# Two FFN and two cross-attention layers on one core: the same steps in another written-out order

## The chip, the core and the metric

The kernel runs on one core of a Trainium2 chip, in one launch. The metric is the device time in microseconds, the median of several runs. TensorE (PE) does the matrix products, VectorE (DVE) and ScalarE (ACT) read PSUM and do element-wise work, GpSimd (POOL) does element-wise work on SBUF alone, and SyncE (SP) issues nearly all transfers. Each engine takes its instructions strictly in the order in which the program lists them; engines meet only through semaphores.

## The reference, cut to what matters

The input x is (16, 128, 128): 16 sequences of 128 tokens with 128 channels, and ctx has the same shape. Four residual layers follow each other, each scaled by the tanh of a gain:

```python
x = x + tanh(g_xattn[0]) * L0_xattn(ctx, ctx, layernorm(x))   # 16 heads of 8, softmax over the heads
x = x + tanh(g_ffn[0])   * L0_ffn(layernorm(x))               # 8 experts of 256, top 2, computed densely
x = x + tanh(g_xattn[1]) * L1_xattn(layernorm(x), ctx)        # both-way attention, then one linear layer
x = x + tanh(g_ffn[1])   * L1_ffn(layernorm(x))               # ternary weights, 8-bit activations, 512 inner
```

## The kernel before

The 16 sequences go in 8 pairs (c from 0 to 7). For every pair the stages are the same, and three or four pairs are in work at a time. The steps have names of the form engine.step, with a number n where a pair has several.

- **First attention (a).** `sp.load_a` loads x and ctx; `dve.a_stats`, `pool.a_rstd` (L843 to L848) and `act.a_norm` normalize; `pe.kq` projects (n = 0 keys, n = 1 queries), after `dve.qkv_lo` and `dve.a_xlo` have made the low parts of the operands. Keys and queries are split into three bf16 parts (`act.part1`, `dve.part_rest`, `act.part2`, `pool.part3` L869), written to DRAM (`sp.store_parts` L791) and fetched back in another layout (`sp.fetch_rows` L799). Four units u follow: `pe.scores`, `dve.head_max`, `dve.head_shift`, `act.head_exp`, `pool.head_sum` (L939, a tree of four additions; two units of pair 0 do it on DVE, L1598), `dve.head_inv`, `pool.head_norm` (L945, in place), then `pe.weighted_v` and `pe.out`.
- **Experts (m).** 16 tiles k: `pe.up` (six matmuls, L1188 to L1190), `act.m_tanh`, `dve.m_u`, then `dve.m_h` or, for the seven odd tiles up to 13, `pool.m_h` (L876); per expert `pe.down` (L1448) and the sum into y (`act.y` with `pool.y` L904 for two experts, `dve.y` for six). m_h is a ring of four buffers.
- **Second attention (f).** A chain of small steps: `dve.f_stats`, `pool.f_rstd`, `act.f_norm`, `pe.f_ct`, `act.f_ct`, `pe.f_scores`, `dve.f_max`, `act.f_exp`, `dve.f_ainv`, `act.f_an`, `pe.f_at`, `act.f_at`, `dve.f_max_max`, `act.f_exp_max`, `pe.f_c2q`, `act.f_c2q`, `pool.f_prod` (L925), `act.f_w4`, `pe.f_z`, `dve.x3`; `pool.y_res` (L912) prepares the residual.
- **Last FFN (g).** `dve.g_stats`, `pool.g_rstd`, ... `act.g_pr`, `act.g_pt`, `pe.g_down`, `act.o_raw`, `pool.out` (L917), `sp.store` (L814).

Once, at the start: weights are loaded (`sp.w_out` is five transfers, the last of them wo_t, L760; then `sp.w_moe`, `sp.w_ffn`, `sp.w_fin`, `sp.w_late`), split into high and low parts (`act.w_hi`, `pool.w_lo`, `dve.w_lo` L1511), and `act.th` (L974) takes the tanh of the gains. `act.th` waits for all five transfers of `sp.w_out`; `dve.bias_parts` (eight instructions, L1521 to L1532) waits for `act.th`. `pe.warm_s`, `pe.warm_f` and `pe.warm_g` are spare matmuls whose results nobody reads.

The order is written out by hand in two tables, WHEN (per pair) and ONCE: every step has a number, and each engine issues its steps in the order of these numbers. The numbers are used for nothing else:

```python
def order(engine):
    ...
    return [(step, n, c) for _, step, n, c in sorted(steps)]
...
for now in order("pool"):
    ...
    if p := due(now, "pool.m_h", n):
```

Of the kernel before, what the change touches and what calls it, by code (L numbers as in the profile page):

```python
# [47 lines left out]
    "sp.load_a": (12, 1501, 2546, 3638, 7464, 12475, 17304, 20931),  # L48
    "sp.store_parts": (
# [6 lines left out]
    ),  # L56
    "sp.fetch_rows": (
        (1960, 3826, 7126, 11165, 15185, 19034, 23535, 27447),
        (2176, 3979, 7280, 10827, 14847, 18694, 23197, 27600),
    ),  # L60
    "sp.load_res": (2646, 5144, 9928, 12576, 16625, 22383, 25012, 28949),
    "sp.load_f": (2697, 11318, 15338, 19216, 24905, 27785, 31537, 34931),
    "sp.store": (16288, 20577, 24859, 28736, 32637, 36238, 38259, 39516),
    "pool.a_rstd": (467, 2292, 3414, 4828, 11299, 16757, 20361, 24484),
    "pool.ct_lo": (399, 2108, 2915, 8603, 12228, 13500, 20286, 21743),
    "pool.part3": (
        (1032, 2533, 6643, 10304, 14257, 18449, 22272, 26895),
        (1821, 3535, 7016, 10717, 14736, 18386, 23086, 27337),
    ),
    "pool.head_sum": (  # L70
# [4 lines left out]
    ),  # L75
    "pool.head_norm": (
# [14 lines left out]
    ),  # L91
    "pool.top_probs": (6705, 10149, 14319, 18585, 22334, 26625, 30788, 33972),
    "pool.y_res": (10367, 13574, 18312, 21817, 25821, 29981, 33448, 36784),
    "pool.f_rstd": (9408, 13378, 17534, 21621, 25895, 30055, 33522, 36662),
    "pool.f_prod": (11082, 15324, 19402, 23525, 27788, 31830, 34983, 37677),
    "pool.g_rstd": (12106, 15779, 20090, 24057, 28227, 32433, 35617, 38044),
    "pool.out": (16206, 20488, 24778, 28655, 32555, 36140, 38177, 0),
    "pool.y": (
        (7460, 11150, 14873, 19328, 23451, 27713, 31905, 34557),
        (7541, 11421, 15250, 19479, 23600, 27862, 32053, 35058),  # L100
    ),
    "act.a_norm": (619, 2451, 3543, 6806, 12380, 17209, 20836, 24936),
# [1712 lines left out]
```

## Time and profile before

| | before |
|---|---|
| time, median of 3 runs | 399.9 us (399.1 to 401.47) |
| span of the profiled execution | 397.3 us |
| what lies around the span, against the median | 2.6 us |
| busy: PE, DVE, POOL, ACT | 82%, 79%, 75%, 65% of the span |
| chain that ended last: PE, POOL, DVE, issue, ACT | 37%, 25%, 13%, 10%, 7% |
| mean granted clock of PE | 0.948 |

The span runs from the first to the last instruction. A busy share is an average over the whole span; the pairs overlap, so the start (until the first scores at 27.7 us), the middle and the end (the last pair alone) have different limits and have to be read apart. The numbers in WHEN and ONCE are in hundredths of a microsecond by their size: the last store has 39516, and the span is 397.3 us.

### The profile page before, as it was taken

The numbers are of one execution on the slowest core, as the hardware profiler recorded it, in microseconds if no ns is written. First come the engines' busy times: TensorE is split into PE (matmuls) and PEld (weight loads), VectorE is DVE, ScalarE is ACT, GpSimd is POOL, SyncE is SP. The second block draws the span as 40 slices with busy tenths as digits, with TensorE's granted clock in tenths as the row PEclk, the third lists the DMA queues.
The fourth block names the chain that finished last, engine by engine and source line by source line (L and its number), as shares of the span: only waits on it lengthen the run. The fifth ranks groups of instructions, "written<-read, shape, count | busy, mean of one in ns | idle before, by whom it ended". The sixth has DMA issues, their size and how long they took to land.

```text
span 397.3 us, 10407 instructions
## 1 busy us (share of the span) xinstructions
PE 324.9 (82%) x3326; PEld 284.0 (71%) x3326; DVE 313.1 (79%) x913; ACT 256.4 (65%) x726; POOL 299.1 (75%) x459
## 2 busy tenths in 40 slices
PE   1365589898999789979998899879978997996875
PEld 1255469787898679867986698669957896994742
DVE  2679877598869997999799979995989678778434
ACT  4335254536846797779667885777658855875754
POOL 4378989799898989898999799988778873443010
PEclk9999767999999999999999999998999999999585
DMA  5967210300341114012401221204100000000000
GB/s 161 289 192 210 81 36 21 116 17 16 88 115 34 29 41 128 19 56 63 108 15 47 68 87 29 61 6 131 33 16 1 28 15 2 2 29 14 2 13 13
DMA packets 34454, 24.17 MB, mean 61 GB/s; under 512 B 3617, under 2 KB 32097, under 8 KB 34401
## 3 DMA queue, kind: packets, MB, share of 16 engines
q1 hardware_dynamic: 33680, 23.32, 19.7%
q8 instruction: 27, 0.44, 0.5%
q10 hardware_dynamic: 720, 0.20, 0.2%
q14 instruction: 27, 0.21, 0.2%
HBM read 16.16 MB, written 7.34 MB: 59 GB/s over the span
## 4 chain that ended last, share of the span: by engine, by line
PE 37%; POOL 25%; DVE 13%; issue 10%; ACT 7%; DMA 4%; SPq 3%; POOLq 0%; DVEq 0%; ACTq 0%
POOL tree L939 9%; PE ps_d L1448 8%; POOL attn L945 8%; PE ps_z L1188 4%; PE ps_a L1196 3%; PE ps_z L1189 3%; PE ps_z L1190 3%; POOL m_h L876 2%; DVE head_max L1584 2%; DMA wf_raw<-in_wd 2%; DVE m_u L1623 1%; DMA k_rows<-rows_dram 1%; DVE y L1655 1%; PE ps_sc L1234 1%; DVE shifted L1590 1%
## 5 line engine op out<-in xcount | busy, mean ns | idle before, releaser
L1188 PE MATMUL ps_z<-m_xhi,w_hi 128*128 128x256 f32 x240 | 76.9, 320 | 12.7 <-DVE m_h L1631 6.1
L945 POOL TENSOR_TENSOR attn<-attn,head_inv 128x1024 f32<-128x1024 f32 x32 | 75.8, 2371 | 0.2 <-DVE head_inv L1606 0.2
L1448 PE MATMUL ps_d<-wdn,m_h 128*128 128x128 f32 x512 | 71.4, 283 | 4.7 <-DVE m_h L1631 2.1
L1448 PEld LDWEIGHTS ps_d<-wdn,m_h 128*128 128x128 f32 x512 | 63.1, 194 | 8.5 <-issue 4.1
L1189 PE MATMUL ps_z<-m_xhi,w_lo 128*128 128x256 f32 x240 | 68.8, 287 | 0.0
L1190 PE MATMUL ps_z<-m_xlo,w_hi 128*128 128x256 f32 x240 | 68.6, 286 | 0.0
L1623 DVE SCALAR_TENSOR_TENSOR m_u<-m_tanh,ps_z 128x256 f32<-128x256 f32 x120 | 49.0, 411 | 17.6 <-ACT m_tanh L1033 16.7
L1033 ACT ACTIVATE m_tanh<-ps_z 128x256 f32<-128x256 f32 x120 | 45.9, 384 | 26.0 <-PE ps_z L1190 25.6
L1188 PEld LDWEIGHTS ps_z<-m_xhi,w_hi 128*128 128x128 f32 x240 | 46.7, 195 | 19.3 <-issue 6.1
L876 POOL TENSOR_TENSOR m_h<-m_u,m_z 128x256 f32<-128x256 f32 x56 | 41.1, 734 | 17.2 <-DVE m_u L1623 17.2
L939 POOL TENSOR_TENSOR tree<-tree 128x256 f32<-128x256 f32 (+2 forms) x90 | 46.4, 515 | 7.1
L1189 PEld LDWEIGHTS ps_z<-m_xhi,w_lo 128*128 128x128 f32 x240 | 46.9, 196 | 0.0
L1190 PEld LDWEIGHTS ps_z<-m_xlo,w_hi 128*128 128x128 f32 x240 | 46.7, 195 | 0.0
L939 POOL TENSOR_TENSOR tree<-attn 128x512 f32<-128x512 f32 x30 | 38.3, 1277 | 6.5 <-ACT attn L1046 6.3
L1584 DVE TENSOR_REDUCE head_max<-ps_sc 128x64 f32<-128x1024 f32 x32 | 38.9, 1215 | 4.5 <-PE ps_sc L1234 4.2
L1046 ACT ACTIVATE attn<-shifted 128x1024 f32<-128x1024 f32 x32 | 33.7, 1055 | 10.1 <-DVE shifted L1590 10.1
L1590 DVE TENSOR_TENSOR shifted<-ps_sc,head_max 128x1024 f32<-128x1024 f32 x32 | 38.8, 1213 | 0.3
L1655 DVE SCALAR_TENSOR_TENSOR y<-ps_d,weights,y 128x128 f32<-128x128 f32 x96 | 28.8, 342 | 4.5 <-PE ps_d L1448 3.1
L1631 DVE TENSOR_TENSOR m_h<-m_u,ps_z 128x256 f32<-128x256 f32 x67 | 27.6, 414 | 5.8 <-PE ps_d L1448 5.1
L1031 ACT ACTIVATE m_z<-ps_z 128x256 f32<-128x256 f32 x53 | 20.2, 381 | 14.6 <-PE ps_z L1190 13.8
L1196 PE MATMUL ps_a<-attn,v_diag 128*32 128x128 f32 x512 | 20.4, 290 | 3.7 <-POOL attn L945 3.3
L1234 PE MATMUL ps_sc<-q_rows,k_rows 48*128 48x64 bf16 x512 | 13.7, 196 | 7.7 <-DVE shifted L1590 5.6
(311 smaller groups left out, 852.0 us busy)
## 6 DMA issues: line engine op xcount, KB each, us to landing
rows_dram<-qk_parts SPq DMA_DIRECT2D x16, 192.0 KB, 2.2
k_rows<-rows_dram SPq DMA_DIRECT2D x16, 192.0 KB
q_rows<-rows_dram SPq DMA_DIRECT2D x16, 192.0 KB
w_raw<-in_w SPq DMA_DIRECT2D x2, 1024.0 KB, 7.9
rows_dram<-qk_parts SPq DMA_DIRECT2D x16, 128.0 KB, 2.0
x_in<-in_x SPq DMA_DIRECT2D x8, 128.0 KB, 2.4
ct_in<-in_ctx_t SPq DMA_DIRECT2D x8, 128.0 KB, 2.4
rows_dram<-qk_parts SPq DMA_DIRECT2D x16, 64.0 KB, 1.7
```

What stands on the lines that cost most here:

```text
L876: pool.tensor_tensor(m_h[:, k % 4], m_u[:, k % 4], m_z1[:, n % 3], ALU.mult).then_inc(s_mhp, 1)
L939: pool.tensor_tensor(dst, src[:, 0:n, :], src[:, n:2 * n, :], ALU.add).then_inc(s_tree, 1)
L945: pool.tensor_tensor(e, e, head_inv[:, u % 2].unsqueeze(1).to_broadcast([P, HEADS, HALF]), ALU.mult).then_inc(s_attn, 1)
L1033: act.activation(m_tanh[:, k % 2], tile_bank(p, k)[:, 0:TOK], ACT.Tanh, scale=0.5).then_inc(s_mt, 1)
L1046: act.activation(attn[:, b, :, k0:k0 + HALF], shifted[:, u % 2], ACT.Exp).then_inc(s_exp, 1)
L1188: pe.matmul(dst, hi_w, hi_x, start=start, stop=False)
L1189: pe.matmul(dst, lo_w, hi_x, start=False, stop=False)
L1190: return pe.matmul(dst, hi_w, lo_x, start=False, stop=True)
L1448: last = pe.matmul(ps_d[:, b * P:(b + 1) * P], m_h[:, m % 4, b * P:(b + 1) * P], wdn[:, m], start=(k == 0), stop=(k == TPE - 1))
L1584: dve.tensor_reduce(head_max[:, u % 2], sc.rearrange("p h k -> p k h"), AX.X, ALU.max).then_inc(s_hmax, 1)
L1590: dve.tensor_tensor(shifted[:, u % 2], sc, head_max[:, u % 2].unsqueeze(1).to_broadcast([P, HEADS, HALF]), ALU.subtract).then_inc(s_shift, 1)
L1623: dve.scalar_tensor_tensor(m_u[:, k % 4], m_tanh[:, k % 2], 1.0, z[:, 0:TOK], ALU.add, ALU.mult).then_inc(s_mu, 1)
```

## The change

Only the numbers in WHEN and ONCE change. Every step, wait, buffer and instruction is kept; on each of the five engines the same list of steps (101 on SP, 226 on POOL, 490 on ACT, 517 on PE, 689 on DVE) is sorted into another order. In words, as far as the prediction speaks of it:

- Start: `act.th` stands ahead of `act.qkv_hi` n = 0 and `act.a_norm` of pair 0, and `dve.bias_parts` ahead of `dve.qkv_lo` n = 0 and 2 and of `dve.a_xlo`. Queries are projected ahead of keys. `sp.w_fin` and `sp.w_late` move behind the fetches of pair 0 and pair 1. On POOL, `pool.a_rstd` of pair 2 and `pool.part3` of pair 1 no longer stand between the first `pool.head_sum` and the first `pool.head_norm`. `dve.w_lo` n = 1 moves from 57.52 to 70.11.
- Middle, on POOL: `pool.part3` of pair 3 (both) and `pool.y_res` of pair 0 stand between `pool.m_h` n = 1 and n = 2 of pair 1; in pairs 3 and 4 a `pool.head_sum` stands between them; `pool.head_norm` n = 3 of pair 6 stands ahead of `pool.m_h` n = 4 of pair 5 and of `pool.g_rstd` of pair 4, behind which it stood.
- End: `act.g_pr` n = 0 and `act.g_tanh` n = 3 of pair 6 move behind `act.f_exp` of pair 7.
- Spare matmuls: seven of `pe.warm_s` at the very start, none between `pe.weighted_v` n = 0 of pair 0 and the middle of that pair's `pe.up`; seven of `pe.warm_f` directly behind the last `pe.down`, none between them and `pe.f_z` of pair 7.

```diff
 WHEN = {
...
     "pool.part3": (
-        (1032, 2533, 6643, 10304, 14257, 18449, 22272, 26895),
-        (1821, 3535, 7016, 10717, 14736, 18386, 23086, 27337),
+        (1641, 2949, 6053, 10610, 13579, 17418, 21932, 25191),
+        (1572, 2879, 6193, 10693, 13881, 18505, 22649, 25857),
     ),
     "pool.head_sum": (
-        (3117, 4949, 8301, 12302, 16280, 20570, 24852, 28729),
-        (0, 5624, 9105, 13076, 17232, 21319, 25518, 29679),
-        (3829, 6030, 9761, 13649, 17656, 21891, 26017, 30177),
-        (0, 7157, 10779, 14947, 18951, 23148, 26958, 31135),
+        (3251, 5069, 8653, 12419, 16440, 20294, 24398, 28083),
+        (0, 5762, 9296, 13163, 17127, 21313, 25260, 28946),
+        (3864, 6263, 9939, 14022, 17677, 22217, 25551, 29499),
+        (0, 7490, 10976, 14686, 18658, 23025, 26992, 30406),
     ),
     "pool.head_norm": (
...
-        (4596, 7995, 11800, 15901, 19859, 24178, 28349, 32128),
+        (4622, 8086, 11783, 15578, 19989, 23740, 27517, 31236),
     ),
     "pool.m_h": (
...
-        (6861, 10441, 14516, 18511, 22765, 26821, 31061, 34325),
-        (7078, 10515, 14799, 18778, 22945, 27399, 31522, 34691),
-        (7615, 11224, 15399, 19254, 23676, 27936, 31979, 35147),
-        (7921, 11495, 15704, 19785, 23982, 28011, 32359, 35331),
+        (6944, 10468, 14543, 18361, 22146, 26375, 30193, 33154),
+        (7208, 10834, 15060, 18948, 22578, 26779, 30264, 33493),
+        (7348, 11407, 15202, 19352, 22869, 26921, 30860, 34201),
+        (7781, 11712, 15812, 19775, 23668, 27750, 31470, 34272),
...
-    "pool.y_res": (10367, 13574, 18312, 21817, 25821, 29981, 33448, 36784),
+    "pool.y_res": (10763, 14472, 18574, 21123, 26628, 29237, 33635, 35725),
...
-    "pool.g_rstd": (12106, 15779, 20090, 24057, 28227, 32433, 35617, 38044),
+    "pool.g_rstd": (12017, 15885, 19657, 23550, 27822, 31541, 34593, 36830),
...
-    "sp.store": (16288, 20577, 24859, 28736, 32637, 36238, 38259, 39516),
+    "sp.store": (16084, 20898, 24336, 28603, 32313, 35876, 37263, 38278),
...
 ONCE = {
...
-    "sp.w_fin": 1005,
...
-    "sp.w_late": 2804,
...
-    "act.th": 851,
...
-    "dve.qkv_lo": (957, 467, 1010),
-    "dve.w_lo": (2176, 5752),
...
-    "dve.bias_parts": 1030,
...
+    "sp.w_fin": 2403,
...
+    "sp.w_late": 4120,
...
+    "act.th": 487,
...
+    "dve.qkv_lo": (910, 463, 929),
+    "dve.w_lo": (2501, 7011),
...
+    "dve.bias_parts": 511,
...
```

## Rows read from the trace of the kernel before

**Rows 1.** Busy time in one stretch of the middle: us, PE, PEld, DVE, ACT, POOL; clock, DMA.
```profile
216.00:256.00 40.00, 36.20 (x391) 31.97 (x390) 35.90 (x110) 30.18 (x90) 36.16 (x55) 1.00 0.22 65
```

**Rows 2.** Busy time of POOL alone in two stretches: length, busy, PE's clock, DMA.
```profile
65.00:270.00 205.00, 186.31 (x281) 1.00 0.20 57
270.00:292.00 22.00, 16.60 (x25) 0.92 0.24 70
```

**Rows 3.** POOL's waits from 46 to 320 us: in total, times, longest us.
```profile
POOL m_h L876 <- DVE m_u L1623: 6.0, 5, 1.8
POOL tree L939 <- ACT attn L1046: 5.1, 7, 1.1
POOL qk_parts L869 <- ACT qk_parts L1022: 3.6, 2, 2.2
```

**Rows 4.** Timeline of SP's queue at the start: start us, us, issue.
```profile
3.66 0.43 SPq L760 DMA_DIRECT2D wo_t<-in_wo  x1
...
21.54 1.35 SPq L799 DMA_DIRECT2D q_rows<-rows_dram  x2
```

**Rows 5.** The tile wo_t, its transfer from issue to landing.
```profile
DMA to landing us min/median/max: 4.8/4.8/4.8
```

**Rows 6.** Timeline of DVE in the start: start us, us, instruction.
```profile
10.26 0.69 DVE L1521 TENSOR_SCALAR bias_raw<-bias_raw,th 96x128 f32<-96x128 f32 x1
...
12.41 0.42 DVE L1532 TENSOR_TENSOR bias_parts<-bias_rest,bias_mid 1x256 bf16<-1x256 f32 x1
...
37.65 1.97 DVE L1598 TENSOR_REDUCE tree<-attn 128x64 f32<-128x1024 f32 x1
...
58.52 1.39 DVE L1511 TENSOR_TENSOR w_lo<-w_raw,w_hi 128x1024 fp32r<-128x1024 f32 x1
```

**Rows 7.** Timeline of PE in the start.
```profile
14.41 0.52 PE L1188 MATMUL ps_a<-a_xhi,wqkv_hi 128*128 128x256 f32 x1
...
27.65 0.46 PE L1234 MATMUL ps_sc<-q_rows,k_rows 48*128 48x64 bf16 x16
```

**Rows 8.** Timeline of POOL in the first attention stage.
```profile
31.80 1.26 POOL L939 TENSOR_TENSOR tree<-attn 128x512 f32<-128x512 f32 x1 [1.28 <-ACT attn L1046]
33.15 1.66 POOL L939 TENSOR_TENSOR tree<-tree 128x256 f32<-128x256 f32 x3
...
36.61 2.37 POOL L945 TENSOR_TENSOR attn<-attn,head_inv 128x1024 f32<-128x1024 f32 x1
...
58.90 2.53 POOL L939 TENSOR_TENSOR tree<-tree 128x256 f32<-128x256 f32 x3
```

**Rows 9.** Timeline of POOL in the middle; in brackets idle time before, and releaser.
```profile
107.76 0.74 POOL L876 TENSOR_TENSOR m_h<-m_u,m_z 128x256 f32<-128x256 f32 x1 [1.01 <-DVE m_u L1623]
...
188.70 0.73 POOL L876 TENSOR_TENSOR m_h<-m_u,m_z 128x256 f32<-128x256 f32 x1 [1.31 <-DVE m_u L1623]
...
228.48 0.73 POOL L876 TENSOR_TENSOR m_h<-m_u,m_z 128x256 f32<-128x256 f32 x1 [1.37 <-DVE m_u L1623]
...
279.98 0.73 POOL L876 TENSOR_TENSOR m_h<-m_u,m_z 128x256 f32<-128x256 f32 x1 [1.80 <-DVE m_u L1623]
281.53 0.19 POOL L843 TENSOR_TENSOR g_rs<-g_mv,eps_col 128x2 f32<-128x2 f32 x1 [0.82 <-DVE g_mv L1493]
...
282.75 2.39 POOL L945 TENSOR_TENSOR attn<-attn,head_inv 128x1024 f32<-128x1024 f32 x1
```

**Rows 10.** Busy time of PE in two stretches: length, busy (matmuls), granted clock, DMA.
```profile
55.10:65.30 10.20, 9.67 (x60) 0.50 0.11 33
65.30:270.10 204.80, 180.87 (x1964) 1.00 0.20 57
```

**Rows 11.** Timeline of DVE in the last pair's second attention.
```profile
368.44 0.22 DVE L1693 SCALAR_TENSOR_TENSOR f_m<-ps_f,bsum,f_nmax 128x1 f32<-128x1 f32 x1
```

**Rows 12.** Timeline of ACT there.
```profile
369.08 0.35 ACT L1096 ACTIVATE f_a<-ps_f,f_nmax 128x128 f32<-128x128 f32 x1
```

**Rows 13.** Timeline at the end: the last two stores, issued by SP.
```profile
394.83 0.82 SPq L814 DMA_DIRECT2D out<-o_sb  x2
```

More of the change, by code:

```diff
@@ L102 @@
-    "act.a_norm": (619, 2451, 3543, 6806, 12380, 17209, 20836, 24936),
-    "act.ct_hi": (340, 2055, 2534, 8320, 9723, 13339, 17931, 21368),
-    "act.a_xhi": (822, 2871, 5804, 9918, 13310, 17762, 21810, 26364),
+        (7279, 10905, 14989, 19020, 22718, 26708, 30709, 33715),
+        (7419, 11336, 15131, 19162, 22798, 26850, 30789, 34130),
+    ),
+    "act.a_norm": (679, 1837, 5049, 8518, 12383, 16339, 19913, 24167),
+    "act.ct_hi": (336, 1457, 2864, 6835, 9864, 14678, 18099, 22144),
+    "act.a_xhi": (848, 2108, 5725, 9636, 13059, 17093, 21630, 24955),
@@ L126 @@
+    "act.m_norm": (5563, 9071, 12939, 16897, 20950, 24847, 28730, 32242),
+    "act.m_xhi": (5697, 9275, 13155, 17043, 21066, 24982, 28807, 32635),
     "act.m_tanh": (
[16 rows of a table removed]
-    ),
-    "act.top_exp": (6437, 9981, 14327, 18048, 22233, 26566, 30878, 34125),
-    "act.f_norm": (9540, 13614, 17679, 21946, 26051, 30231, 33652, 36792),
-    "act.f_ct": (9759, 13840, 17967, 22153, 26222, 30453, 33841, 36918),
-    "act.f_exp": (10217, 14157, 18330, 22490, 26492, 30766, 34200, 37176),
-    "act.f_an": (10363, 14349, 18511, 22640, 26775, 31003, 34336, 37309),
@@ new lines @@
+    "act.top_exp": (6420, 10017, 14188, 17914, 21975, 26063, 29783, 32886),
+    "act.f_norm": (9789, 13587, 17614, 21321, 25208, 29448, 32809, 35734),
+    "act.f_ct": (9942, 13741, 17783, 21555, 25515, 29587, 32984, 35823),
+    "act.f_exp": (10258, 14030, 18131, 22015, 25894, 29882, 33347, 36012),
+    "act.f_an": (10363, 14200, 18240, 22176, 26003, 29991, 33505, 36094),
+    "act.f_at": (10526, 14413, 18445, 22339, 26167, 30154, 33681, 36194),
+    "act.f_exp_max": (10649, 14793, 18653, 22559, 26196, 30280, 33778, 36245),
@@ L156 @@
+    "act.f_c2q": (11026, 15029, 18930, 22868, 26503, 30523, 34014, 36406),
+    "act.f_w4": (11127, 15247, 19103, 23040, 27045, 30930, 34130, 36466),
+    "act.g_norm": (12144, 16013, 20163, 23677, 27949, 31719, 34782, 36957),
+    "act.g_r": (12489, 16243, 20337, 24374, 28239, 31986, 34910, 37168),
+    "act.g_qt": (13032, 16825, 20786, 25014, 28484, 32319, 35198, 37315),
     "act.g_tanh": (
[4 rows of a table removed]
[4 rows of a table added]
     ),
     "act.g_pr": (
-        (14413, 18108, 22704, 27012, 30533, 34037, 37029, 38752),
-        (15510, 19430, 23653, 27490, 31635, 35192, 37774, 39102),
+        (14442, 17925, 22897, 26797, 30729, 33204, 36532, 37585),
+        (15160, 19248, 23255, 27104, 31018, 34189, 36782, 37907),
@@ L209 @@
     "pe.up": (
[16 rows of a table removed]
[16 rows of a table added]
     ),
-    "pe.gate": (5784, 9616, 13576, 17651, 21651, 25789, 30049, 33850),
+    "pe.gate": (6006, 9403, 13995, 17239, 21528, 25265, 29318, 32740),
     "pe.down": (
[8 rows of a table removed]
-    ),
-    "pe.f_ct": (9683, 13767, 17883, 22050, 26149, 30375, 33765, 36851),
-    "pe.f_scores": (9978, 13938, 18062, 22280, 26317, 30548, 33989, 36991),
-    "pe.f_at": (10437, 14429, 18637, 22942, 26854, 31083, 34431, 37359),
-    "pe.f_c2q": (10839, 14988, 19118, 23275, 27450, 31440, 34833, 37574),
[8 rows of a table added]
+    ),
@@ L242 @@
+    "pe.f_ct": (9898, 13695, 17737, 21437, 25300, 29541, 32921, 35788),
+    "pe.f_scores": (10077, 13831, 17872, 21695, 25703, 29681, 33091, 35891),
+    "pe.f_at": (10435, 14324, 18356, 22251, 26078, 30065, 33593, 36140),
+    "pe.f_c2q": (10915, 14918, 18783, 22696, 26392, 30411, 33903, 36330),
     "pe.f_z": (
-        (11234, 15326, 19457, 23614, 27702, 31672, 35092, 37700),
-        (11293, 15401, 19532, 23745, 27931, 32016, 35224, 37805),
+        (11319, 15512, 19178, 23127, 27347, 30950, 34257, 36462),
+        (11365, 15559, 19225, 23173, 27394, 31004, 34304, 36555),
@@ new lines @@
+    "dve.f_max": (10188, 13959, 18025, 21926, 25823, 29810, 33216, 35958),
+    "dve.f_ainv": (10343, 14165, 18218, 22142, 25981, 29969, 33434, 36064),
+    "dve.f_max_max": (10569, 14610, 18582, 22493, 26211, 30198, 33726, 36228),
+    "dve.f_q2c": (11005, 15167, 19061, 22942, 26552, 30888, 34045, 36312),
+    "dve.x3": (11521, 15758, 19427, 23330, 27550, 31165, 34466, 36690),
+    "dve.g_amax": (12255, 16105, 20261, 24016, 28086, 31855, 34874, 37049),
+    "dve.g_clamp": (12302, 16138, 20294, 24049, 28118, 31888, 34907, 37082),
```

182 lines of the change are left out of this document (82 added, 100 removed), and 250 rows, old and new, of the table WHEN.

## The prediction, on record before the changed kernel ran

> **What bounds the kernel now.** I read the busy time by stretches first, because the shares of the whole span mix a start, a middle and an end with different limits. In the middle a pair costs about 40 us, and in such a stretch PE, DVE and POOL are each busy for 36 of the 40 us [rows 1]; ACT is not. So no engine alone is the limit. Three engines at 90% hand work to each other through small rings of buffers, and what an order can save is the remaining tenth. Next I read POOL alone: 186.3 us of 205.0 before 270 us (91%), but only 16.6 of 22.0 (75%) from there to 292 us [rows 2]. That is the worst place of the middle. Then POOL's waits from 46 to 320 us: the largest is `m_h`, which waits for DVE's `m_u`, 6.0 us in 5 times [rows 3]. In the timeline I looked up what stood behind POOL at each of them, since that is what an order can put in front. Outside the middle, the start until the first scores and the last pair's chain are read step by step. The clock comes last: PE runs at full clock through the middle and at half from 55.1 to 65.3 us [rows 10].
>
> The rows are of an execution with a span of 397.3 us. The median of the runs shown is 399.9 us, so 2.6 us are taken as lying around the span, before and after alike. I sum differences, and add them to 399.9. With runs from 399.1 to 401.5, 0.5% (2.0 us) is about what can be told from no change.
>
> **The change, part by part.** No instruction goes or comes, so each part is a wait that ends earlier or later.
>
> *Start, until the scores.* `act.th` waits for wo_t, issued at 3.66 us and landed 4.8 us later, at 8.5 [rows 4, 5]. The transfers ahead of it on SP are the same in both orders. ACT now stands at this wait with `a_norm` behind it, and DVE with `bias_parts`, and behind that the low parts that both projections need. `bias_parts` lasts from 10.26 to 12.83 us, 2.6 us [rows 6]; from about 8.7 on that ends at 11.3. Three short DVE steps of about 0.3 us each (estimate, by the last rows of `bias_parts`) end at 12.2. From the start of the queries' projection to the queries' fetch it took 21.54 - 14.41 = 7.1 us [rows 4, 7]. Now the keys, which were far ahead before, go through the same path together with the queries: one more projection, four more steps of ACT, DVE and POOL, three more stores. Their cost lies between nothing and another 7.1 us; I take 3.4, about half, since the two share each engine by turns. The queries' fetch is issued at 12.2 + 7.1 + 3.4 = 22.7 us instead of 21.54. Scores follow it by 27.65 - 21.54 = 6.1 us [rows 4, 7]: 28.8 us, +1.2. The moved `w_fin` cannot give this back, because the stores now wait for the parts and not for SP's queue.
>
> *From the scores to the end of pair 0's attention.* The first tree went from 31.80 to 33.15 + 1.66 = 34.8 us, but `head_norm` began only at 36.61 [rows 8], since two other steps of POOL stood between. They are moved away, and the 1.2 us are won back there. The two sums on DVE take 1.97 us each [rows 6]; with the later start the second `head_norm` waits for the first of them, about 0.5 us. So +0.5 at the end of this stage. The steps that were moved away must still be done: they go where POOL was waiting for ACT's exponentials, a wait of 0.9 us among those of [rows 3]. I take +0.7 for the start as a whole; the bounds are -2.2 (the keys cost nothing) and +4.9 (they cost 7.1).
>
> *The port.* While DVE subtracted `w_lo` (58.52, 1.39 us [rows 6]), POOL's three additions from 58.90 took 2.53 us; the same three took 1.66 us elsewhere [rows 8]. That is 0.9 us, and POOL had work waiting behind. The new order puts this subtraction after the first expert tiles, near a pause of POOL. I take -0.9, bounds 0 and -0.9. The Trainium skill (SBUF — State Buffer, section "Who interferes with whom") says that a DVE instruction with two SBUF inputs and a GpSimd instruction that reads SBUF exclude each other, the later one waiting for the whole of the earlier; the rows agree. By that rule the 0.9 us go only if the subtraction meets a true pause of POOL, and otherwise move to another POOL step; then this term is 0 and the sum below ends at 395.8. In the middle no large DVE step has two SBUF inputs, since they read PSUM, so nothing more is to be had there.
>
> *The middle.* Four places, each a wait of `m_h` on DVE. In pair 5, POOL waited 1.80 us at `m_h` and 0.82 us at `g_rstd`, with `head_norm` (2.39 us) standing behind both [rows 9]. The new order puts `head_norm` ahead of both, and it fits into the 2.6 us almost exactly: -2.6. In pairs 1, 3 and 4 the waits are 1.01, 1.31 and 1.37 us, 3.7 together [rows 9]. What is put in front there is longer than the wait (a whole tree, two parts and a residual), so `m_h` and with it `pe.down` come later, and PE and DVE, themselves busy for 90%, lose a part of what POOL wins. I take half, -1.8. Bounds for the middle: 0, if PE and DVE bring back every wait elsewhere, and -14.7, the sum of the three rows of [rows 3]. I stay at -4.4, nearer to the first, because only these places could be traced to a swap. What the other moved steps do there I put at 0 for want of a row; it lies within these bounds.
>
> *The end.* In pair 7 `f_m` of the first half was ready at 368.44 + 0.22 = 368.66 us, and `f_exp` began at 369.08 [rows 11, 12], because `g_pr` and `g_tanh` of pair 6 stood in front on ACT. They move behind it: -0.4. The rest of the chain is the same small steps, each waiting for the one before. Bounds: +1.0 (below) to -3.
>
> *PE's clock.* The granted clock was at half from 55.1 to 65.3 us although spare matmuls stood in front [rows 10]; the new order has none between the first `weighted_v` and the middle of the first experts, and none in the last pair's chain before `f_z`. A matmul took 9.67 / 60 = 0.16 us of PE at half clock and 180.87 / 1964 = 0.09 at full [rows 10], with somewhat different mixes. If `f_ct` and `f_scores` also run at half, the last chain gains about 1 us of length. I take 0 for both places, since the dense `up` matmuls brought the clock back by themselves at 65.3. The Trainium skill (TensorE: Matmul & The Clock Gate, section "HAM oscillation — how this bites in real kernels") says that a gap in PE's work puts the clock back to half, so that the next burst starts slowly. That speaks against this change.
>
> **The sum:** +0.7 - 0.9 - 4.4 - 0.4 = -5.0 us, and 399.9 - 5.0 = 394.9 us.
>
> **The rivals.**
> - *The whole order works as its numbers read.* They are sort keys and no measurement, and no term above comes from them. But the last store had the key 39516, and the trace issued it within 394.83 to 395.65 us [rows 13]; the new key is 38278, 12.4 us less: 387.5 us. This needs all of POOL's named waits in the middle (14.7 us in [rows 3]) to shrink by most of their length, and the start not to be late. For it: 90% on three engines leaves that much room. Against it: the start, where the key of `act.th` (4.87 us) lies ahead of the landing at 8.5.
> - *The waits come back on the other engines.* Where a tree of 3.0 us [rows 8] fills a wait of 1.31 or 1.37 us, `m_h` is 1.7 and 1.6 us later than before; in pair 1 it is 1.1, with three steps of about 0.7 us (estimate, by the 0.74 of `m_h`) in a wait of 1.01. That is 4.4 us in all, and it reaches the end as far as the ring of four buffers has no slack. If half does, the three places give +2.2 in place of -1.8, and the sum is 394.9 + 4.0 = 398.9 us: the same within 0.5%. For it: PE and DVE at 90% [rows 1]. Against it: PE had no long wait there that is put down to POOL.
> - *Slower: the half clock lasts longer.* Place: from the first `weighted_v` to the middle of pair 0's experts, where no spare matmuls are left. At 0.16 - 0.09 = 0.07 us for each matmul, 100 more matmuls at half clock cost 7 us, and 399.9 - 5.0 + 7.0 = 401.9 us. It decides from about 100 matmuls, near two thirds of pair 0's `up` and `down`. For it: the clock was low there even with the spare matmuls [rows 10]. Against it: the dense experts raised it before.
>
> **How the numbers follow.** My forecast (390.5 to 397.9, all faster by over 0.5%) has a chance of 0.44, the whole order 0.24, the returning waits 0.20, the slow clock 0.12. Faster by over 0.5%: 0.44 + 0.24 = 0.68; within 0.5%: 0.20; slower: 0.12. The predicted time is that of the likeliest, 394.9 us. The range goes from 387.0, just below the whole order's 387.5, to 401.5, which leaves out about half of the slow-clock case and what may lie under the whole order's time: some 0.15 together. The forecast's own range is 390.5 to 397.9.
>
> **What would show it right or wrong.** Start: `act.th` near 8.5 us, `bias_parts` until 11.3, the first scores near 28.8; scores at 27.7 or earlier would refute the term. Port: DVE's second `w_lo` beside a pause of POOL, and no tree addition group of 2.5 us. Middle: POOL from 270 to 292 us as dense as before 270; `m_h` waits under 3 us in all; if instead PE's waits for `m_h` grow, the second rival is right. End: `f_exp` directly behind `f_max`. Clock: the first full-clock stretch of pair 0's experts beginning near 65 us; at 72 or later, the third rival. The prediction is wrong if the pairs of the middle come to 39 us or less each (the whole order), or if the start loses more than 2 us and the middle gains nothing.

## The result, and the profile after

The new order is slower: 417.25 us (runs of 413.76 to 419.14) against 399.5 us of the kernel before on the same chip, a ratio of 1.0439 with a 95% interval of 1.0395 to 1.0484. The forecast was 394.9 us, and the range ended at 401.5.

The page first: engine, busy us, share of the span, instructions. The upper fence is the kernel before, the lower the one after.

```profile
PE 324.9 (82%) x3326; PEld 284.0 (71%) x3326; DVE 313.1 (79%) x913; ACT 256.4 (65%) x726; POOL 299.1 (75%) x459
```
```profile
PE 329.8 (80%) x3323; PEld 291.0 (70%) x3326; DVE 328.4 (79%) x913; ACT 257.4 (62%) x726; POOL 296.3 (72%) x459
...
PEclk9996558889999989999999899999999999999688
...
PE 52%; DVE 23%; issue 11%; ACT 9%; POOL 2%; DMA 1%; SPq 1%; DVEq 0%; ACTq 0%; POOLq 0%
```

Two things stand out. DVE's 913 instructions are busy for 15.3 us longer, though an order can't make an instruction longer by itself. Added up one by one they are 10.5 us longer (377.6 us against 367.1); the rest of the 15.3 us is that neighbours overlap less. And in the slices from 31 to 62 us the clock is at 5 and 6 tenths. In the chain of waits POOL fell from 25% to 2%: it is no longer what the others wait for.

Where the time goes is seen from one step that each pair does once, the statistics after its experts (the first `f_st` in DVE's timeline), in us from the start of the span:

| pair | 0 | 1 | 2 | 3 | 5 | 7 |
|---|---|---|---|---|---|---|
| before | 94.6 | 133.6 | 172.9 | 213.4 | 297.7 | 363.4 |
| after | 103.1 | 149.0 | 191.0 | 231.7 | 315.4 | 381.0 |
| later by | 8.5 | 15.4 | 18.1 | 18.3 | 17.7 | 17.6 |

The whole loss is made in pairs 0, 1 and 2. From there on the lag neither grows nor shrinks.

Nearly all of DVE's growth is in a handful of small instructions. Groups by line (busy us, mean ns), before and then after:

```profile
L1664 DVE TENSOR_SCALAR w_first<-expert_no,top_nof,tprob 128x8 f32<-128x8 f32 x16 | 4.9, 303 | 0.4 <-POOL tprob L894 0.4
L1664 DVE TENSOR_SCALAR w_second<-expert_no,top_nof,tprob 128x8 f32<-128x8 f32 x16 | 4.5, 282 | 0.0
```
```profile
L1664 DVE TENSOR_SCALAR w_second<-expert_no,top_nof,tprob 128x8 f32<-128x8 f32 x16 | 9.0, 562 | 0.0
L1664 DVE TENSOR_SCALAR w_first<-expert_no,top_nof,tprob 128x8 f32<-128x8 f32 x16 | 7.9, 492 | 0.0
...
L1750 DVE TENSOR_SCALAR g_q<-g_r 128x256 bf16<-128x256 f32 (+1 forms) x9 | 4.9, 557 | 1.8 <-ACT g_r L1143 1.5
...
L1645 DVE CAST top_nof<-top_no 128x16 f32<-128x16 uint32 x8 | 3.4, 421 | 0.0
```

L1664 works on 8 columns, and takes 16.9 us in place of 9.4. The timeline of pair 0's four of them shows why. DVE after, then POOL after:

```profile
74.49 1.48 DVE L1664 TENSOR_SCALAR w_first<-expert_no,top_nof,tprob 128x8 f32<-128x8 f32 x1
75.89 0.78 DVE L1664 TENSOR_SCALAR w_second<-expert_no,top_nof,tprob 128x8 f32<-128x8 f32 x1
76.58 0.77 DVE L1664 TENSOR_SCALAR w_first<-expert_no,top_nof,tprob 128x8 f32<-128x8 f32 x1
77.27 0.28 DVE L1664 TENSOR_SCALAR w_second<-expert_no,top_nof,tprob 128x8 f32<-128x8 f32 x1
77.46 1.21 DVE L1511 TENSOR_TENSOR w_lo<-w_raw,w_hi 128x1024 fp32r<-128x1024 f32 x1
```
```profile
73.57 2.37 POOL L945 TENSOR_TENSOR attn<-attn,head_inv 128x1024 f32<-128x1024 f32 x1
75.90 1.43 POOL L876 TENSOR_TENSOR m_h<-m_u,m_z 128x256 f32<-128x256 f32 x2
79.56 0.73 POOL L904 TENSOR_TENSOR y<-y_raw,x 128x256 f32<-128x256 f32 x1 [2.23 <-ACT y_raw L1074]
```

The first ends at 75.97, just behind `attn` (75.94); the second and the third end one `m_h` apart (76.67, 77.35), as POOL's two instructions do. The fourth meets an idle POOL and takes 0.28 us. So each of these instructions waits for the POOL instruction that is running, and three of them in a row wait three times. (The wait lies inside the instruction's own time and not at a semaphore: that engines meet only through semaphores, as said ahead of the prediction, does not hold here.) In the kernel before, the same four took 0.28 us each, from 70.89 on, and POOL stood idle just then, from 70.27 to 72.47. DVE's first of the four, and POOL's next instruction:

```profile
70.89 0.28 DVE L1664 TENSOR_SCALAR w_first<-expert_no,top_nof,tprob 128x8 f32<-128x8 f32 x1
...
72.47 0.68 POOL L869 TENSOR_TENSOR qk_parts<-qk_rest,qk_parts 128x256 bf16<-128x256 f32 x1 [2.20 <-ACT qk_parts L1022]
```

This is the longest of the `qk_parts` waits of [rows 3]. The new order did away with it, and so with the gap that DVE's small steps had been using. The chain of waits runs through them: start us, us, what.

```profile
73.50 1.08 DVE shifted L1590
74.57 1.40 DVE w_first L1664
75.97 0.69 DVE w_second L1664
76.67 0.69 DVE w_first L1664
...
78.60 0.17 DVE weights L1669
...
79.12 0.37 ACT y_raw L1074
...
79.62 2.06 PE ps_d L1448 x8
```

PE's second `down` product waits for it, and then takes 2.06 us for 8 products; at 87.32 the same takes 0.89. That is the clock, read from the stretches (us, PE, PEld, DVE, ACT, POOL busy with counts, granted clock, DMA):

```profile
34.87:65.59 30.72, 20.99 (x235) 16.87 (x237) 22.85 (x38) 11.27 (x22) 25.07 (x30) 0.50 0.31 91
65.59:79.24 13.65, 8.42 (x99) 7.55 (x93) 11.18 (x28) 7.23 (x20) 9.28 (x14) 1.00 0.42 116
79.24:86.07 6.83, 5.77 (x25) 5.54 (x26) 1.72 (x5) 1.25 (x4) 4.72 (x7) 0.50 0.00 0
...
216.00:256.00 40.00, 34.37 (x377) 31.48 (x375) 35.46 (x102) 29.42 (x87) 33.37 (x51) 0.96 0.21 60
```

At half (1.2 GHz) are 30.7 us in one piece, in place of two pieces of 6.8 and 10.2 before [rows 10 for the second]; and another 6.8 in the middle of pair 0's experts, which begins while PE stands idle for 2.5 us, until that `down` product starts at 79.62. In the stretch of [rows 1] POOL has 33.37 of 40 us where it had 36.16.

The other marks that the prediction named. The start, on SP and on PE:

```profile
22.00 1.35 SPq L799 DMA_DIRECT2D q_rows<-rows_dram  x2
```
```profile
24.44 5.02 PE L1213 MATMUL ps_f<-ident_bf 128*128 128x128 bf16 x56
29.39 0.41 PE L1234 MATMUL ps_sc<-q_rows,k_rows 48*128 48x64 bf16 x16
```

`act.th` ran at 8.50, `bias_parts` ended at 10.98 (11.3 was expected), the queries' fetch is issued at 22.0 (22.7 expected; 21.54 in [rows 4]), and the scores come at 29.39 (28.8 expected; 27.65 in [rows 7]), straight behind 14 groups of four spare products.

POOL's waits, from 46 to 338 us, beside [rows 3]; and pair 5's place, beside [rows 9]:

```profile
POOL m_h L876 <- DVE m_u L1623: 7.6, 5, 3.4
POOL tree L939 <- ACT attn L1046: 6.6, 5, 1.4
POOL y L904 <- ACT y_raw L1074: 6.0, 5, 2.2
```
```profile
300.76 0.73 POOL L876 TENSOR_TENSOR m_h<-m_u,m_z 128x256 f32<-128x256 f32 x1
301.45 0.20 POOL L843 TENSOR_TENSOR g_rs<-g_mv,eps_col 128x2 f32<-128x2 f32 x1
```

Pair 5's two waits are gone, as traced: both steps follow `attn` with no idle time in brackets. But `m_h` waits longer in all than before, where under 3 us was expected, and a wait of `y` for ACT has come up that was not there. PE's waits for `m_h`, the sign of the second rival, add up to 9.2 us in place of 8.5 (6.9 in the first experiment below): no growth that would carry this loss. At the end `f_exp` stands directly behind `f_max`, as expected: it waits for `f_m` alone (beside [rows 11, 12]).

```profile
386.28 0.37 ACT L1096 ACTIVATE f_a<-ps_f,f_nmax 128x128 f32<-128x128 f32 x1 [0.62 <-DVE f_m L1693]
```

### The profile page after: what moved, and what is told of

It reads as the page before. It is cut to its first block, busy times and chain, and to the rows that moved or that the text cites. A ratio compares the mean times of both kernels' runs of the same rounds, so it can differ in the third digit from the quotient of the medians.

```text
span 413.9 us, 10404 instructions
## 1 busy us (share of the span) xinstructions
PE 329.8 (80%) x3323; PEld 291.0 (70%) x3326; DVE 328.4 (79%) x913; ACT 257.4 (62%) x726; POOL 296.3 (72%) x459
## 4 chain that ended last, share of the span: by engine, by line
PE 52%; DVE 23%; issue 11%; ACT 9%; POOL 2%; DMA 1%; SPq 1%; DVEq 0%; ACTq 0%; POOLq 0%
PE ps_d L1448 13%; PE ps_z L1188 7%; PE ps_z L1189 5%; PE ps_z L1190 5%; DVE head_max L1584 3%; DVE shifted L1590 2%; DVE y L1655 2%; DVE m_u L1623 2%; DVE m_h L1631 2%; PE ps_a L1196 2%; PE ps_sc L1234 2%; DVE w_second L1664 1%; DVE w_first L1664 1%; PE ps_f L1213 1%; DMA wo_t<-in_wo 1%
## 5 line engine op out<-in xcount | busy, mean ns | idle before, releaser
L1448 PE MATMUL ps_d<-wdn,m_h 128*128 128x128 f32 x512 | 72.8, 287 | 9.4 <-ACT y_raw L1074 5.4
L1448 PEld LDWEIGHTS ps_d<-wdn,m_h 128*128 128x128 f32 x512 | 64.7, 198 | 13.1 <-issue 10.1
L1189 PE MATMUL ps_z<-m_xhi,w_lo 128*128 128x256 f32 x240 | 69.7, 291 | 0.0
L1190 PE MATMUL ps_z<-m_xlo,w_hi 128*128 128x256 f32 x240 | 69.5, 290 | 0.0
L1623 DVE SCALAR_TENSOR_TENSOR m_u<-m_tanh,ps_z 128x256 f32<-128x256 f32 x120 | 48.2, 412 | 15.7 <-ACT m_tanh L1033 14.9
L939 POOL TENSOR_TENSOR tree<-tree 128x256 f32<-128x256 f32 (+2 forms) x90 | 45.4, 504 | 7.1
L1189 PEld LDWEIGHTS ps_z<-m_xhi,w_lo 128*128 128x128 f32 x240 | 47.8, 199 | 0.0
L1190 PEld LDWEIGHTS ps_z<-m_xlo,w_hi 128*128 128x128 f32 x240 | 47.7, 199 | 0.0
L1655 DVE SCALAR_TENSOR_TENSOR y<-ps_d,weights,y 128x128 f32<-128x128 f32 x96 | 28.8, 341 | 4.1 <-PE ps_d L1448 3.5
```

Of the source, the lines that this page charges most:

```text
L939: pool.tensor_tensor(dst, src[:, 0:n, :], src[:, n:2 * n, :], ALU.add).then_inc(s_tree, 1)
L1189: pe.matmul(dst, lo_w, hi_x, start=False, stop=False)
L1190: return pe.matmul(dst, hi_w, lo_x, start=False, stop=True)
L1448: last = pe.matmul(ps_d[:, b * P:(b + 1) * P], m_h[:, m % 4, b * P:(b + 1) * P], wdn[:, m], start=(k == 0), stop=(k == TPE - 1))
L1623: dve.scalar_tensor_tensor(m_u[:, k % 4], m_tanh[:, k % 2], 1.0, z[:, 0:TOK], ALU.add, ALU.mult).then_inc(s_mu, 1)
L1655: dve.scalar_tensor_tensor(y[:, b], ps_d[:, b * P:(b + 1) * P], weights[:, b, n:n + 1], y[:, b], ALU.mult, ALU.add).then_inc(s_y, 1)
```

## The experiments

Four candidates for 17.7 us: the port (DVE's and POOL's instructions in each other's way at SBUF), PE's clock, the start, and the order as such (what stands in front of what, port and clock aside). Ratios are to the kernel before, run beside each on the same chip (398.2 to 399.0 us); the one of after is 1.0439, and 0.01 is 4 us.

**The port alone.** If L1664 waits because its form takes a port that POOL needs too (where this theory comes from is said further down), then another form should not wait. The only edit is the shape: 3 rows of 3 with a gap are read, and 9 in a row are written; the sum behind it reads 8 of the 9. `w_second` gets the same shape as `w_first`. The ninth column is no expert and is not used.

```diff
-        expert_no = sb("expert_no", [P, EXPERTS])
+        expert_no = sb("expert_no", [P, 3, 4])
-        w_first = sb("w_first", [P, 2, EXPERTS])
+        w_first = sb("w_first", [P, 2, 9])
-            pool.iota(expert_no[:], pattern=[[1, EXPERTS]], base=0, ...
+            pool.iota(expert_no[:], pattern=[[3, 3], [1, 4]], base=0, ...
-                            dve.tensor_scalar(dst[:, b], expert_no[:], ...
+                            dve.tensor_scalar(dst[:, b], expert_no[:, :, 0:3], ...
```

> The order of after, with the 32 instructions of L1664 in another form: the expert numbers lie in 3 rows of 3 with a gap (9 columns read instead of 8), so that the operand read and the operand written differ in shape and the instruction needs one SBUF port instead of two. Nothing else differs. Port theory: in after, L1664 took 16.9 us against 9.4 before, single ones 1.3 to 1.5 us against 0.28, because DVE waited for POOL's instruction to end; the chain of waits runs through them. They then take about 0.29 us each again, 9.5 us in all, and 4 to 7.5 of the 17 us come back: 410 to 413 us. Rival, order alone: DVE's lost time there is slack, and the time stays at 416 to 418 us though L1664 is short. If L1664 stays near 0.53 us on the mean, the shape is not what takes the second port and the run tells nothing of the price.

Measured: 410.33 us, ratio 1.0288 (1.0248 to 1.0329).

```profile
L1664 DVE TENSOR_SCALAR w_first<-expert_no,top_nof,tprob 128x9 f32<-128x9 f32 x16 | 4.4, 273 | 0.0
L1664 DVE TENSOR_SCALAR w_second<-expert_no,top_nof,tprob 128x9 f32<-128x9 f32 x16 | 4.4, 272 | 0.0
```

The subtraction behind them, in DVE's timeline:

```profile
75.44 1.78 DVE L1511 TENSOR_TENSOR w_lo<-w_raw,w_hi 128x1024 fp32r<-128x1024 f32 x1
```

All 32 take 0.27 us now, and 1.5 points of the 4.4 are gone. The subtraction, still with two SBUF inputs, takes 1.78 in place of 1.21 us: it inherits a part of the wait. The clock can have given little of this: in the trace it is at half for 30.7 us between 36 and 71 us, as in after for 30.7, and near 80 us for 3.4 in place of 6.8. The port theory holds, with its size. That the form matters through a port, and not in another way, is the theory's reading; the runs show the wait and that the form ends it.

**The same form in the old order**, as a control.

> The order of before, untouched, with L1664 alone in the one-port form (no spares added). A control for the form: in the order of before these instructions waited 0.4 us in all, so if the gain of 6.9 us in the order of after came from the port and not from the form as such, nothing changes here: 398 to 399.5 us, ratio 0.995 to 1.003. If the form gains by itself, it is under 396.

Measured: 397.94 us, ratio 0.9992 (0.9963 to 1.0021). No change: the form itself gains nothing where little collides, so the gain above comes from the collisions.

**The late half of the weights.** `w_lo` ran between the weights and their sum (77.46).

```diff
-    "act.w_hi": (1962, 1518, 6249, 1612),
+    "act.w_hi": (1962, 1518, 5430, 1612),
-    "dve.w_lo": (2501, 7011),
+    "dve.w_lo": (2501, 5850),
```

> The order of after with two steps moved back: the high half of the up weights on ACT from key 62.5 to 54.3 (after its v_diag of pair 1) and the low half on DVE from key 70.1 to 58.5 (after the a_xlo of pair 2). In after the low half ran at 77.46 between weights (end 77.55) and the sum of the weights (78.60), for which ACT's y and the second down product waited. Theory that this step is a part of the loss: pair 0's second half of experts starts 1.2 us earlier or more (up8 81.1 or before, in place of 82.3), and 1 to 2.5 us of it last to the end: 414.5 to 416 us. Rival, DVE is not late there: 417 us. Slower would mean that the moved steps now stand before the first products of pair 0's experts.

Measured: 415.97 us, ratio 1.0414 (1.0354 to 1.0475), within the interval of after. `w_lo` ran at 62.80, but the weights began 1.5 us later (76.01) and collided with POOL as before:

```profile
62.80 1.36 DVE L1511 TENSOR_TENSOR w_lo<-w_raw,w_hi 128x1024 fp32r<-128x1024 f32 x1
...
76.01 1.49 DVE L1664 TENSOR_SCALAR w_first<-expert_no,top_nof,tprob 128x8 f32<-128x8 f32 x1
77.41 0.78 DVE L1664 TENSOR_SCALAR w_second<-expert_no,top_nof,tprob 128x8 f32<-128x8 f32 x1
```

That theory falls by its mark: up8 started at 81.95, 0.4 us earlier and not 1.2. The time lies in the range given for it, but also in that of no change.

**The clock.** 70 more groups of spares (4 products each) in PE's gaps, in the order of after:

```diff
-    "pe.warm_s": (271, ..., 9876),
+    "pe.warm_s": tuple(sorted((271, ..., 9876) + (3149,) * 9 + (3398,) * 12 + (4225,) * 14 + (4524,) + (4683,) * 2
+        + (4956,) * 3 + (5040, 5168) + (5652,) * 5 + (5701,) * 2 + (6297,) * 4 + (6610,) * 2 + (6760,) * 4 + (7215,) * 10)),
```

> The order of after plus 70 more groups of spare products on PE (4 of 128 columns each) between 31.5 and 72.2 of the key time, so that PE has work in its gaps there. Clock theory: in after the granted clock was half from 34.87 to 65.59 us and from 79.24 to 86.07; with the gaps filled it is full in most of the first stretch, each product of 0.21 us there takes 0.14 or less, and 2.5 to 5 us come back: 412 to 414.5 us. Rival: the products of that stretch wait for DVE and POOL anyway, the clock changes and the time stays within 1 us of 417; or the spares stand in the way and it is slower.

Measured: 409.88 us, ratio 1.0284 (1.0239 to 1.0328). That is more than the 2.5 to 5 us expected. L1664 still takes 16.9 us. The clock is full throughout both stretches, and pair 0's statistics come at 96.4 in place of 103.1 us:

```profile
34.87:65.59 30.72, 26.81 (x455) 23.37 (x453) 25.22 (x46) 14.09 (x29) 27.67 (x34) 1.00 0.38 106
...
79.24:86.07 6.83, 6.79 (x69) 6.13 (x68) 5.61 (x12) 3.03 (x9) 6.59 (x7) 1.00 0.01 2
```

Where the 6.7 us arise, from the two traces: the first weighted values start at 45.62 in both, so up to there the full clock, net of the spares in front, gave nothing. At the statistics ahead of the experts this kernel is 1.6 us ahead (54.52 against 56.10), at the first `up` 2.9 (59.46 against 62.38), and the experts give the other 3.8.

**The old spares in their old places**, none added.

```diff
-    "pe.warm_s": (271, ..., 4224, 6759, 8188, 9130, 9152, 9831, 9853, 9876),
+    "pe.warm_s": (2027,) * 5 + (2769,) * 2 + (3083,) * 5 + (3396,) * 3 + (3744,) * 7 + (4245,) * 13 + (4683,)
+        + (5928,) * 2 + (6297,) * 4 + (7306, 7687, 9152, 9831, 9853, 9876),
```

> The order of after, with its 48 groups of spare products not added to but put back in front of the steps that they stood in front of in before (13 ahead of the first weighted_v, 1 ahead of its third, 2 ahead of pair 1's last scores, 4 ahead of up4). Clock theory in the narrow form (it is the moved spares that cost): the clock is full again for part of 35 to 65 us, and 3 to 7 us come back: 410 to 414 us. Rival: moved spares alone change little, since the real products are also spread otherwise: 416 to 418 us.

Measured: 419.06 us, ratio 1.0525 (1.0462 to 1.0589). No gain, and slower than either case of the expectation. The clock did change:

```profile
34.87:44.30 9.43, 6.36 (x100) 5.99 (x96) 8.69 (x13) 2.62 (x3) 7.63 (x7) 1.00 0.27 72
44.30:64.80 20.50, 15.72 (x156) 12.03 (x157) 13.76 (x25) 7.90 (x19) 16.24 (x22) 0.50 0.37 104
78.50:85.30 6.80, 5.60 (x27) 5.33 (x28) 2.00 (x7) 1.63 (x5) 4.20 (x6) 0.50 0.00 0
```

9.4 us of pair 0's attention at full clock bought nothing; what stayed at half was the rest of that attention and the first experts (`up` from 61.79). So putting the moved spares back is not enough. That the real products are also spread otherwise, and the old number of spares no longer fills the gaps, is argued; the run fits it.

**Pairs 0 and 1 by the old keys, the others by the new** (shifted by 1.2 us).

> Pairs 0 and 1 and all that is done once by the keys of before, pairs 2 to 7 by those of after (shifted by 1.2 us to join them). The lag of after behind before at the statistics that follow the experts was 8.5 us in pair 0, 15.4 in pair 1, 18.1 in pair 2 and 17.6 in pair 7. Theory that the loss is made in the first two pairs (the start, the port, the clock there): about 15 of the 17 us are gone, 400 to 403 us. Rival, the new order is worse in every pair and the first ones only show it first: each of six pairs loses some 2 us and it is 408 us or more. If the new order of the later pairs gains by itself, it is under 399 us.

Measured: 429.51 us, ratio 1.0786 (1.0748 to 1.0825), worse than either order. Pair 0, by its old keys, was 8.7 us late at its statistics, and L1664 took 13.5 us in all. The joint is a third order with losses of its own, which were not followed up, and the run tells nothing of the two.

**Port and clock together.**

> The order of after with both edits: the 32 instructions of L1664 in the form that needs one SBUF port (alone: 410.3 us, 6.9 us less than after on the median) and the 70 added groups of spare products (alone: 409.9, 7.4 less). If port and clock are separate losses they add up: 14 us back, 402 to 404 us. If each was the cover of the other (the chain waits for whichever is later), it stays at 407 us or more.

Measured: 406.18 us, ratio 1.0213 (1.0140 to 1.0286). Alone they gave back 1.51 and 1.55 points, together 2.26: less than the sum of 3.06, and more than either, but the interval reaches those of each alone. In the executions that were traced, the lag at pair 7's statistics is 17.6 us in after, 11.8 with the form, 11.2 with the spares and 6.1 with both, nearly the full sum (11.5 of 12.3 us). Whether the two add up in full or in part stays open.

**And the start.** Added to that: `act.th` at key 851 and `bias_parts` at 1030, as in the old table.

> As the kernel with both edits, and also the two steps of the start by the keys of before: act.th (the five small transfers, wo_t last at 8.5 us) behind the first a_xhi, and dve.bias_parts behind the first a_xlo. In after ACT's a_norm of pair 0 was 2.3 us later than before and the first scores 1.7 us later. Theory that the start is a third loss that lasts: 1.2 to 1.7 us less than with both edits alone, first scores at 28 us or earlier. Rival: the first scores wait for pair 0's fetched rows, later by another reason, and nothing changes.

Measured: 404.29 us, ratio 1.0169 (1.0110 to 1.0228), 1.9 us less, but in an interval that overlaps the one before it. ACT's `a_xn` starts at 6.79 again (8.81 in after), yet the first scores come at 29.02 and not at 28, straight behind the spares again:

```profile
25.76 3.33 PE L1213 MATMUL ps_f<-ident_bf 128*128 128x128 bf16 x42
29.02 0.41 PE L1234 MATMUL ps_sc<-q_rows,k_rows 48*128 48x64 bf16 x16
```

The steps that wait for wo_t were not what made the scores late. With fewer spares in front and these steps still early (the kernel with the old spares in their old places) the scores came at 27.96.

**The rest of the port, and the spares ahead of the scores.** In pair 1's stretch other small DVE steps had waited for POOL; `g_q` took 2.35 us beside an `attn` of POOL. They get other forms, and 7 groups of spares go behind the scores. The main lines:

```diff
-                    dve.tensor_copy(top_nof[:], top_no[:]).then_inc(s_tnof, 1)
+                    dve.tensor_copy(top_nof[:].rearrange("p (a c) -> p a c", a=3),
+                                    top_no[:].rearrange("p b n -> p (b n)")[:, 0:12]
+                                    .rearrange("p (a c) -> p a c", a=3)[:, :, 0:3]).then_inc(s_tnof, 1)
-                    dve.scalar_tensor_tensor(g_sc[:, :, 2], g_amc[:], cg[:, 1:2], g_amc[:], ALU.mult,
-                                             ALU.mult).then_inc(s_gsc, 1)
+                    dve.tensor_scalar(g_sc[:, 0, 2:3], g_amc[:, 0:1], cg[:, 1:2], g_amc[:, 0:1], ALU.mult, ALU.mult)
+                    dve.tensor_scalar(g_sc[:, 1, 2:3], g_amc[:, 1:2], cg[:, 1:2], g_amc[:, 1:2], ALU.mult,
+                                      ALU.mult).then_inc(s_gsc, 1)
+                        g3 = slice(0, 3) if p.first else both(g)
-                        dve.tensor_scalar(g_q[:, both(g)], g_r[:, both(g)], ROUND, 127.0, ALU.subtract,
+                        dve.tensor_scalar(g_q[:, g3, 0:P], g_r[:, g3], ROUND, 127.0, ALU.subtract,
```

`g_r` has a third row for it, and `g_q` rows with a gap; in pair 0 the third row is rounded too and not used.

> As the kernel with port, spares and start (404.3 us), with the other DVE instructions that waited for POOL there put in a form that should need one SBUF port: the cast of the expert numbers (1.07, 0.56 and 0.45 us over its 0.16 in pairs 1, 3 and 4), the scales of the last FFN (0.9 over 0.2 in pair 0; two of one element each) and, in pair 0 alone, the rounding g_q (2.1 over 0.23; 384 elements in 3 rows). Besides, 7 of the 14 groups of spares that stand ahead of the first scores go behind them, since these groups ran until 29.4 us though the rows had landed at 28.0. Port theory: pair 1 loses 6.4 us between the statistics of pair 0 and its own there, of which 4 lie in these instructions; 2 to 5 us come back: 399 to 402 us. Rival, order: the chain of pair 1 waits elsewhere, and it stays at 403 to 405 us.

Measured: 400.58 us, ratio 1.0046 (1.0010 to 1.0082). `g_q` of pair 0 takes 0.54 us, the casts 0.16; the first scores come at 27.17.

```profile
L1645 DVE CAST top_nof<-top_no 128x9 f32<-128x9 uint32 x8 | 1.3, 162 | 0.0
```

Pair 1's statistics go from 140.7 to 137.5 us. How the 1.2 points against the kernel before this one divide between the forms and the spares was not run apart.

**The old order with both findings.** One-port form of L1664, and spares in PE's gaps: 27 groups early, 18 and 27 in the last pair's chain (72 in all; the expectation says 64).

> The order of before, untouched, with L1664 in the one-port form and 64 more groups of spare products in PE's gaps (27 between 41 and 58 us, 18 between 363 and 372, 27 of them and the rest between 382 and 391). What the two findings on after say of the old order: L1664 loses only 0.4 us there, and the half clock stretches of before are 44.9 to 51.7, 55.1 to 65.3, 369.1 to 379.4 and 386.2 to 396.4 us. If the clock is worth there what it was worth in after (7.4 us for 30.7 us), 2 to 5 us: 394 to 397 us. Rival: in the tail the products wait for the chain of the last pair and only the first stretch pays: 397 to 398; or the spares stand in the way: 399 or more.

Measured: 394.78 us, ratio 0.9922 (0.9893 to 0.9952): faster than both kernels. From 366 us to its end the clock is 0.98; before, it was 0.64 from 369 us on. The last store is issued at 389.3 in place of 394.8 [rows 13]; 2 us of that were already there in pair 7's statistics (361.4), the rest came in the tail. The traced execution was the fastest of its ten (393.65 us).

```profile
366.00:392.00 26.00, 19.65 (x128) 11.26 (x127) 12.18 (x45) 17.19 (x48) 2.78 (x7) 0.98 0.04 11
```

**Its early spares alone.**

> The order of before with the 27 groups of spares between 41 and 58 us alone (no other form of L1664, none in the tail). The old order with all three edits took 394.8 us; its trace put 1.6 us of the gain ahead of pair 0's statistics and 3 us in the tail. So 1 to 2 us less than before here, 396.5 to 398, ratio 0.994 to 0.999. Rival: the tail's gain needs the early clock or is chance, and this one alone has all of it (395) or none (399).

Measured: 397.31 us, ratio 0.9978 (0.9946 to 1.0010): as expected, though not told from no change. That the tail's spares give the rest is argued from the trace; they were not run alone.

**The new order with all of it**: the kernel with the rest of the port, and 55 more groups of spares from 362 us on.

> The order of after with all edits of the kernel before this one (one-port forms, spares, start: 400.6 us) and 55 more groups of spares in PE's gaps of the last pair, from 362 us on, as the old order got in its tail. The old order with its one-port form and spares early and in the tail took 394.8 us (ratio 0.992), of which its trace put 3 us in the tail. If the tail pays as much here, 397 to 398.5 us, and the new order, with its port and clock losses out, is still 2 to 4 us behind the old one with the same edits; if the new order is as good as the old one, 395 us; if the tail pays nothing here, 400 to 401.

Measured: 399.77 us, ratio 1.0021 (0.9988 to 1.0055). The spares in the tail are not told from none here (1.0046 before them). With every loss taken out that was found, the new order is as fast as the old one was without any edit, and about 1% behind the old one with like edits (0.9922). What that 1% is was not found.

## Why the prediction was wrong

*The port: the step that failed.* The prediction gave -0.9 and said that "nothing more is to be had there", because no large DVE step of the middle has two SBUF inputs. It asked only where a collision could be won, and only of large steps. It did not ask which small steps had no collision because POOL was waiting, and which would get one when the wait is filled. What it asked for came: `w_lo` ran at 77.46 in a pause of POOL, and no group of additions took 2.5 us. What it left out cost about 6 us: the term was not -0.9 but some +5. The rows were there: L1664 on 8 columns at 0.28 us, in the middle of a POOL wait of 2.2 us. Even a small step that did collide stood in [rows 6]: `bias_raw` at 10.26 took 0.69 us, while POOL ran

```profile
10.14 0.73 POOL L869 TENSOR_TENSOR qk_parts<-qk_rest,qk_parts 128x256 bf16<-128x256 f32 x1 [3.70 <-ACT qk_parts L1022]
```

and in after, at 8.81 with POOL idle, 0.28 us. In the new order L1664 took 7.5 us more, all DVE instructions together 10.5 more, and taking the collisions out of L1664 alone gave 1.5 points (6 us). The Trainium skill (SBUF — State Buffer, section "Who interferes with whom") has the rule in full: besides an instruction with two SBUF inputs, copies, casts and `tensor_scalar` in a two-port mode exclude GpSimd too, and whichever is second waits for all of the first. The prediction used the first half of it and not the second; the timeline at 74.49 us agrees with the second. The Trainium skill (VectorE: DVE Perf Modes, section "What auto-detection actually checks") gives the condition for that mode, outermost counts that are both even or equal; the one-port form breaks it, with 3 against 9, and the 0.27 us of all 32 instructions agree.

*PE's clock: the second.* "I take 0 for both places" left out about 6 us at the first place (1.55 points for the added spares alone; 0.75, not told from nothing, with the form already in). For the second place 0 was right: from pair 7's statistics to the end it takes 33.0 us in after and 33.9 before. The third rival had the place and nearly the price (0.07 us for each matmul, about 100 matmuls), and got a chance of 0.12. Its test was badly chosen: the first full-clock stretch did begin near 65 us (65.59), yet the half clock had begun at 34.87 in place of 44.9, and came back at 79.24, when PE waited for DVE's weights. That L1664's collisions lengthen this second piece is not shown: it lasts 3.4 and not 6.8 us without them, but also 3.4 with them, in the kernel with the late half of the weights moved. The argument that dense `up` products bring the clock back by themselves held at 65.6 and failed at 79.2. The rule of the Trainium skill that the prediction quoted against the change (TensorE: Matmul & The Clock Gate, section "HAM oscillation — how this bites in real kernels") agrees: at 79.24 the clock fell while PE stood idle for 2.5 us, and with spares in the gaps it stayed full.

*The start: size a little off, cause not as worked out.* +0.7 was forecast for the stage, and the scores came 1.7 us late and not 1.2. The queries' fetch was 0.5 us late, better than worked out. The rest was spares: 14 groups (56 products) stood ahead of the scores and ran from 24.44 to 29.46 us, where before there were 7 (28 products). Until 28.0 us one started every 0.107 us, from there every 0.055; the clock's own record begins at 28.0. The prediction looked at spares that were taken away, and not at where they had gone.

*The middle and the end: right where traced.* Pair 5's waits went away, and `f_exp` moved up. From pair 3 on the new order loses nothing; but it wins nothing either while collisions last. Once L1664 has the other form, it does win. The lag behind before at the statistics of pair 2 and of pair 7, in us, one execution each:

| kernel (new order) | pair 2 | pair 7 | won between |
|---|---|---|---|
| after | 18.1 | 17.6 | 0.5 |
| spares | 11.6 | 11.2 | 0.4 |
| form of L1664 | 15.7 | 11.8 | 3.9 |
| form and spares | 10.0 | 6.1 | 3.9 |
| and the start | 10.2 | 4.4 | 5.8 |
| and the rest of the port | 5.5 | -1.3 | 6.8 |
| and spares in the tail | 7.1 | 1.5 | 5.6 |

The two other kernels of the new order with L1664's old form lose a little over 1 us there; the old order with the form alone wins 0.3. So a gain of about the -4.4 us of the middle is in the new order; the collisions hid it, and the losses of pairs 0 to 2 outweighed it. That it comes from the four places that the prediction named is not shown.

*Why 4.4% slower and not 5 us less.* In ratios: 1.0439 of after; 1.0213 without L1664's collisions and with the clock kept up; 1.0169 with the start (not told apart); 1.0046 without the other collisions and with half of the spares behind the scores. What is left is 0.5% against the old order as it was, and 1% where both have like edits; no run says what it is.

## What to carry to other kernels

A gap on one engine can be what another one runs in. Before an order fills POOL's waits, list the DVE instructions that run inside them, the smallest included, and ask of each whether all its operands lie in SBUF, as those that waited here had; such a one can wait for the rest of the POOL instruction that it meets, however small it is (0.28 us became 1.48 here), and if others follow in a row, each waits anew. And when spare products are moved, look both at the place that they leave and at the one where they go: in the one the clock falls, in the other they delay the first real product behind them.

## What the runs showed of the hardware

A DVE instruction on 8 columns took 0.28 us with POOL idle and up to 1.49 us beside a POOL instruction; `g_q` took 2.35 us, from 142.08 to 144.43, while POOL's `attn` ended at 144.28. The work of L1664 in a shape of 3 rows against 9 columns took 0.27 us on the mean in all seven kernels that had it, in either order, and none of the 224 took more than 0.29. Half clock cost nothing that could be measured in pair 0's attention up to the first weighted values (10.7 us of it). The rest of it, until pair 0's statistics, cost 6.7 us by the traces with and without added spares: 2.9 ahead of the experts and 3.8 in them.
